# The source-row gathers of a graph attention kernel read their indices from the whole table instead of a per-chunk copy

## The reference, cut to what matters

```
src, dst = (edge_index[0], edge_index[1])
q = (x @ Wq + bq).reshape(n, H, D)
k = (x @ Wk + bk).reshape(n, H, D)
v = (x @ Wv + bv).reshape(n, H, D)
qi = q[dst]
kj = k[src]
vj = v[src]
alpha = jnp.sum(qi * kj, axis=-1) / jnp.sqrt(jnp.float32(D))
m = jax.ops.segment_max(alpha, dst, num_segments=n)
ex = jnp.exp(alpha - m[dst])
denom = jax.ops.segment_sum(ex, dst, num_segments=n)
a = ex / (denom[dst] + 1e-16)
out = jax.ops.segment_sum(a[..., None] * vj, dst, num_segments=n)
```

## Time and profile before

| | |
|---|---|
| median of 3 runs | 1489.38 us (1484.93 to 1494.15) |
| time of the profiled execution | 1499.95 us |
| its span, first to last instruction | 1498.1 us |
| mean granted TensorE clock | 0.932 of full speed |
| edge stage, first gather to the last tiles (71 to about 845 us) | about 774 us |
| all that follows | about 653 us |

### The profile page before, as it was taken

The page is one execution under the profiler, slowest core; times in us unless marked ns, Lnnn a source line. Parts: engine busy times, 40 slices in busy tenths (PEclk is TensorE's granted clock), DMA queues, the critical chain, the costliest instruction groups (busy, mean ns, idle before and its releaser), DMA issues. The chain is left out here.

```text
span 1498.1 us, 24128 instructions
## 1 busy us (share of the span) xinstructions
PE 1242.9 (83%) x6835; PEld 959.2 (64%) x6835; DVE 1068.4 (71%) x2557; ACT 807.4 (54%) x2534; POOL 927.2 (62%) x883
## 2 busy tenths in 40 slices
PE   7988776676776766667767889999999999999999
PEld 3444544444444444444445558889888998999998
DVE  7646877777778776768767888877766655656655
ACT  1365766666667666566655845556443244344443
POOL 3365666666666656666666546776676567667665
PEclk9998889999889898789887989999999999999999
DMA  7476766666666666666666030110100000000002
GB/s 225 164 229 203 224 201 171 194 196 191 186 184 203 185 187 178 182 183 181 185 178 179 8 105 29 29 50 12 30 22 15 8 22 15 8 22 15 1 12 76
DMA packets 74072, 175.40 MB, mean 117 GB/s; under 512 B 11500, under 2 KB 36651, under 8 KB 73945
## 3 DMA queue, kind: packets, MB, share of 16 engines
q0 software_dynamic: 37632, 124.28, 29.4%
q1 hardware_dynamic: 34641, 48.25, 10.0%
q10 hardware_dynamic: 1672, 1.33, 0.3%
HBM read 159.91 MB, written 13.91 MB: 116 GB/s over the span
## 5 line engine op out<-in xcount | busy, mean ns | idle before, releaser
L691 POOL DMA_INDIRECT ring<-kv_rows,idx x464 | 469.0, 1011 | 297.0 <-issue 116.6
L765 ACT ACTIVATE ring<-ring 128x64 f32<-128x64 f32 x1800 | 442.1, 336 | 15.0 <-issue 13.2
L1291 POOL TENSOR_TENSOR wm<-k_gf,wm 128x512 fp32r<-128x512 f32 (+2 forms) x224 | 258.9, 1159 | 144.1 <-DVE wm L1792 144.1
L1390 ACT ACTIVATE k_gf<-psF,k_scT 128x512 f32<-128x512 f32 (+2 forms) x224 | 162.1, 724 | 252.2 <-PE psF L1561 248.9
L811 PE MATMUL psA<-ring,oh 128*128 128x260 f32 x912 | 276.7, 432 | 7.1 <-DVE k_acc L1017 6.1
L785 PE MATMUL psQ<-k_q,ohT 128*128 x1392 | 228.6, 305 | 60.7 <-issue 56.0
L1792 DVE CAST wm<-k_gf 128x512 fp32r<-128x512 f32 (+2 forms) x224 | 159.5, 719 | 155.8 <-ACT k_gf L1390 155.8
L983 DVE TENSOR_TENSOR prod<-psQ,ring 128x512 f32<-128x512 f32 x232 | 157.6, 679 | 110.6 <-remote 68.5
L785 PEld LDWEIGHTS psQ<-k_q,ohT 128*128 128x128 bf16 x1392 | 131.8, 105 | 119.8 <-issue 88.7
L811 PEld LDWEIGHTS psA<-ring,oh 128*128 128x128 f32 x912 | 179.8, 219 | 35.8 <-ACT ring L765 6.5
L1023 DVE TENSOR_REDUCE alpha<-prod 128x8 f32<-128x512 f32 x232 | 155.8, 672 | 0.2
(11 more groups left out here) (284 smaller groups left out, 2607.3 us busy)
## 6 DMA issues: line engine op xcount, KB each, us to landing
ohT<-step_destinations SPq DMA_DIRECT2D x29, 512.0 KB
ring<-kv_rows,idx POOLq DMA_INDIRECT x464
kv_rows<-kvst SPq DMA_DIRECT2D x25, 260.0 KB, 2.6
we<-in_L_ffn_W SPq DMA_DIRECT2D x16, 256.0 KB, 2.7
residual<-qst SPq DMA_DIRECT2D x25, 128.0 KB
xs<-in_x SPq DMA_DIRECT2D x2, 1024.0 KB, 9.1
resin<-residual SPq DMA_DIRECT2D x4, 512.0 KB
we<-in_L_ffn_Wo SPq DMA_DIRECT2D x8, 256.0 KB, 2.8
```

Source lines behind the costliest of these rows:

```text
L691: nc.gpsimd.indirect_dma_start(out=ring[:, LT * (j % CP) + k, j // CP:j // CP + 2, :].rearrange("p t e -> p (t e)"), out_offset=None, in_= ...
L765: last = nc.scalar.activation(row[:, 0:D], row[:, 0:D], ACT.Copy, scale=row[:, D:HW_])
L1291: nc.gpsimd.tensor_tensor(low[:, i % 2, m, 0:w], gf[:, n % 4, 0:w], high[:, i % 2, m, 0:w], ALU.subtract).then_inc(s_gl, 1)
L1390: nc.scalar.activation(gf[:, n % 4, 0:cols(g)], ps, ACT.Relu, bias=bias, scale=scale).then_inc(s_ev, 1)
```

## The change

The gathers name their index column in the whole table `k_srcI`, column `LT * step + k`, instead of a column of the copy. The tile `idx`, the function `places`, its 29 activations, the semaphore `s_idx` and the two waits (POOL's for the copy, ACT's for the landed gathers) are gone. All else in the program is as it was; tiles allocated behind `idx` lie 128 bytes lower in each partition.

```
-        idx = sb("idx", [P, 2, W], I32)
...
-                cc, par = CR * i + j // CP, j // CP % 2
-                if j % CP == 0:
-                    pool.wait_ge(s_idx, cc + 1)
...
-                        in_offset=bass.IndirectOffsetOnAxis(ap=idx[:, par, LT * (j % CP) + k:LT * (j % CP) + k + 1], axis=0)
+                        in_offset=bass.IndirectOffsetOnAxis(ap=keep["srcI"][:, LT * step + k:LT * step + k + 1], axis=0)
...
-            def places(cc, par, fresh):
-
-                if not fresh:
-                    act.wait_ge(s_kv[CP - 1], 16 * LT * (cc - 1))
-                nc.scalar.activation(idx[:, par, :], keep["srcI"][:, bass.ds(W * cc, W)], ACT.Copy).then_inc(s_idx, 1)
...
-            places(0, 0, True)
...
-                if j % CP == 1 and live(i, j - 1, fresh, -CP):
-                    places(CR * i + j // CP + 1, (j // CP + 1) % 2, fresh and j < CP)
```

More of the change, by code:

```diff
@@ L592, in attend @@
         s_set = sem("s_set")
-        s_idx, s_stc = sem("s_idx"), sem("s_stc")
+        s_stc = sem("s_stc")
         s_kv = [sem(f"s_kv{k}") for k in range(CP)]
```

## The result

The changed kernel takes 1479.59 us (median of 8 runs, 1478.32 to 1481.59), the kernel before, beside it, 1491.72 us (8 runs, 1484.93 to 1495.19). The ratio is 0.9933, 95% interval 0.9910 to 0.9957: faster by 0.67%, where 1.23% was forecast. It is the 0.67% that this document has to explain: the two profiled executions differ by just what was forecast, 1498.1 us of span before and 1478.5 us after, 19.6 us less. The 1479.59 us lie at the upper edge of the forecast's own range, 1461 to 1480 us, and the gain falls where the prediction had put 0.44 (within 1%), not where it had put 0.46 (over 1%).

The account below looks back on a forecast made before the run. A ring of waits, paced by POOL's runs and pauses, was taken to bound the 774 us edge stage. Only DVE's 19 us counted: 1499.95 to 1481 us, ratio 0.9873, so 1471 us on the median; range 1461 to 1480 us.

Parts of the forecast that it names:

- POOL's pauses as the clock of the stage: Edge stage: POOL's runs of eight gathers (10.0 us) and a pause, four steps done, set the pace of the ring.
- The waits replaced by shorter ones: Chunk starts: without the index wait, a pause of 3.99 us becomes one like those of 1.94 to 2.37 us.
- The price by POOL: POOL's 17 index waits, 55.2 us: twelve long ones give 23.0 us, five others 4.3 us, sum 27 us.
- The sign that was to mean wrong: Profile after: runs of ten and more gathers with DVE chunks of over 28 us beside them would refute the prediction.
- The gather price: POOL's gathers from the 464-column table: still 0.946 us in the median, no gain or loss taken.
- the ACT copies: ACT's 29 index copies of 0.20 us go: 5.8 us, costed at nothing, worth 5.8 us at most.
- the data: DVE's wait before its product: gathered data isn't late, so an earlier gather gives DVE nothing directly.
- the 19 us: Edge stage by DVE's walk: all 28 chunks at 25.20 us in place of 25.89, 28 x 0.69 us shorter.
- Effect and cause the other way round: Rival: DVE, PE and ACT are slow for another reason, the index wait only shows it; 1483 to 1490 us, chance 0.29.
- The rule of the Trainium skill: Only the DVE/GpSimd port pair contends, so gathers can't hold PE or ACT; POOL's pauses would be effect, shorter ones give nothing.
- Longer runs, slower kernel: Rival: without index waits POOL's runs lengthen and others wait; 12 chunks paying 3.7 us give 1514 us, chance 0.10.
- The dearer table: Rival: the wide table costs 0.05 us more a gather, 23 us on POOL; 1493 us, chance 0.07.

Follow-up runs that it names:

- late copy: Kernel before, with ACT's index copy one place later, behind eight more activations, POOL's wait kept: 1546.10 us, ratio 1.0403, where the kernel before took 1487.36 us.
- table alone: Kernel before, gathers reading the whole table, copy and waits kept: ratios 1.0004, 1.0005, 0.9991 (before about 1350 us) and 0.9987 (1484.92 us, before 1485.18).

## Why the direction was right and the size was not

**POOL's pauses as the clock of the stage: borne out where a wait is made longer.** The doses of the wait are 0, 38.8, 55.2 and 127.2 us, and DVE's chunk goes 24.78 to 25.13, 25.36, 25.89 and 27.31 us with them; one profile each, and the steps below 127.2 us, 0.23 and 0.53 us, are of the size of the 0.35 us between profiles of the changed kernel. The late copy's chunk is made up of POOL's rows: 16 gathers of 0.986 us in the mean with 0.30 us between them are 20.6 us, and its pauses behind the first gather, 185.0 us, are 6.6 us a chunk, 27.2 us in all.

**The waits replaced by shorter ones: right.** The price by POOL took the sum to be there 1.9 us before a gather that waited for the copy; behind step 24, DVE's addition of that sum began 1.35 to 1.53 us ahead of all ten such gathers of over 1.2 us of wait, so it was there at least that much earlier. At the starts of the chunks after, the pauses are 2.4 us at most, but for 4.99 us at the start of chunk 1, which had been 4.66 us for the copy. Of the 55.2 us, (96.0 + 42.5 + 5.8) - (62.2 + 35.4 + 13.4) = 33.3 us came back in other waits (35.4 and 13.4 us are PE's and the remote ones of before), under the 35 us of the forecast, and 6.0 us more as issue (122.6 against 116.6). The idle time fell by 16.5 us, not by the 20 us or more that was forecast; but of the pauses over 1.2 us, 148.7 - 127.5 = 21.2 us went, between DVE's 19 and POOL's 27. DVE's chunks were to be near 25.2 us from end to end, with no series of 27 us. The mean is right (25.13 us), and the series is gone, but the evenness isn't there: single chunks of 27.2 to 28.3 us remain, four of 28, where there were seven of 27.0 us or more. The sign that was to mean wrong, a run of ten with a chunk of over 28 us beside it, stands there once, at the second chunk.

**The gather price, the ACT copies, the data: right.** The median is 946 ns from either index tile (949 ns in the table alone), and the table alone measures 1.00 in both forms, in four sets.

**The step that failed is the 19 us, read from one execution and carried over as a ratio.** The prediction took 28 x 0.69 us from the profiled execution, made 1499.95 us into 1481, called it 0.9873, and applied that to the median of the runs, which gave 1471. As a statement on that execution it was right: 1480.36 / 1499.95 is 0.9869. But 1499.95 us wasn't a usual execution of the kernel before. It is 8.2 us over the median, and above all eight runs; the changed kernel's profiled execution, 1480.36 us, is 0.8 us over its own. Take the 8.2 us from 19.6, add the 0.8, and 12.2 us are left: the 12.1 us that was measured. That the long waits which made up the term were in part what made this execution a slow one fits this, but isn't shown: the kernel before was profiled only once in this form. The table alone, with all waits in place and a profiled time of 1483.19 us close to its median, shows what is more usual: waits of 3.7 us or more only five times, not twelve, and 28 x (25.36 - 25.12) = 7 us of chunk length over the change beside it. So in place of the 19 us the runs showed 12.1 us between the medians, beside 19.6 us between the two profiled executions. That the latter hit the forecast is in part luck: the other two profiles of the changed kernel (1480.1 and 1462.8 us) lie 18.0 and 35.3 us under the profile of before. It is luck too that the forecast's own absolute value, 1481 us for the changed kernel, is 0.1% off.

Even so there is no one true size. The same comparison gave 12.1, 18.1 and 3.2 us in three sets. The changed kernel itself took 1464.62 to 1472.97 us in one of them and 1478.32 to 1481.59 us in another, with no run in common. How often a chunk has a wait of 3.7 us or more differs too (twelve and five times in the two profiles with the wait in its old place), and that what the change can give differs with it is a guess.

**The rivals.** *Effect and cause the other way round* (1483 to 1490 us) falls by the late copy: an edit that adds no work and only puts the copy one place later costs 4%, where the rival expected 1.00. The rule of the Trainium skill behind it, page "SBUF — State Buffer", section "Who interferes with whom", isn't contradicted by that. What falls is what I drew from it. The runs show that POOL's pauses carry over to DVE through the waits between them; they don't show that a gather holds another engine. *Longer runs, slower kernel* (1514 us) falls: of the three profiles of the changed kernel the one with the most runs of ten or more, 20, is the fastest, with the smallest sum of pauses. The chunk that the rival was built on did stay slow, 28.3 us (29.63 before), with a run of ten gathers beside it; it is one chunk at the start. *The dearer table* (1493 us) falls by the 946 ns and by the ratios of the table alone.

**What stays open.** First, what makes the 1490 form, where POOL pauses about every eight gathers. The traces show one side of it. ACT's `nrow` waits for PE's second transpose (L818 before, L805 in the changed kernel). In the kernel before, the transpose that the `nrow` at 586.02 waited for was over at 582.52, and ACT was idle:

```profile
582.25 0.27 PE L818 MATMUL psM<-k_ident,stc 128*64 128x128 f32 x1
```

The same pair in the 1350 form (table alone):

```profile
400.80 0.27 PE L818 MATMUL psM<-k_ident,stc 128*64 128x128 f32 x1
```

```profile
401.10 0.27 ACT L750 ACTIVATE nrow<-psM 64x128 f32<-64x128 f32 x1 [2.38 <-PE psM L818]
```

3.50 us lie between end and start in the one, 0.03 us in the other. In the 1350 form all 29 `nrow` begin 0.03 to 0.04 us behind the transpose. In the kernel before, in the 1490 form, 13 of 29 come 1.0 to 5.1 us behind it, each with ACT idle, and each of these 13 begins in a pause of POOL or behind its last gather, 1.1 to 1.5 us after the gather before it had ended. In the changed kernel 14 of 29 come 1.5 to 4.6 us late, but six of these while POOL is still gathering. So PE's signals do arrive late in the 1490 form, often only in a pause of POOL; but a run of gathers is not enough to make them late, since in the 1350 form 416 gathers go one after the other and none is. (The ends of PE's instructions are modelled in the profile.) The cause isn't shown.

Second, whether in that form POOL's wait alone is what the change gains by. Set directly beside the table alone in their common set, the change is 3.0 us faster by the medians and 3.3 us by the means, with a standard error of 1.1 us: taking away copy and waits gains something there with the table already in place. ACT's own wait never held it, as said above, so of ACT's part only the 29 copies are left, 5.8 us of work; the gains of 12.1 and 18.1 us are more than that, the 3.2 us aren't. The late copy speaks for POOL's wait, but the runs that would part the two in the 1490 form all fell in the 1350 form. Nor was it tested there whether the tiles that lie 128 bytes lower in the changed kernel matter; in the 1350 form the change, with them, is at 0.9990. Nothing tried beats the changed kernel.

## What to carry to other kernels

A wait on a pacing queue for a copy of data that the engine could read where it lies can cost far more than the copy: here 0.20 us of work behind waits of up to 6 us, and 4% when the copy slipped by one place; and nothing measurable in the form in which the queue hardly waits. The size of such a gain is no property of the kernel alone: set the profiled execution beside the median before carrying a ratio over, and if it is the slowest of all, take the excess off the term first (here 19 - 8.2 = 10.8 us, for 12.1 us measured). Before a wait is put down to the engine that the profile names, look whether the very step that the wait needs had not ended long before. In a ring of waits, sum what is left of each pause and not what is removed: of 55 us taken away, 33 us came back in the waits for others.

## What the runs showed of the hardware

The same kernel takes 1350 or 1490 us. The tail is alike, 653 us at a granted clock of 0.98 (of 2.4 GHz) in both. The edge stage is 626 us at a clock of 0.98 in the profile of the table alone, and 754 to 774 us at 0.88 to 0.89 in those of the kernel before and after (739 us at 0.89 in the fastest profile of the changed kernel), with DMA moving 231 GB/s or 187 to 196 GB/s. Over the whole execution the mean clock of the kernel before is 0.98 to 0.99 in the one form, but for one run, and 0.92 to 0.95 in the other. The lower clock alone isn't the difference: PE's busy time in the stage is 497 us against 551 to 556 us, 54 to 59 us more, while the stage differs by 129 to 148 us, and POOL, which has 472 to 476 us of work in either, shows it as pauses. And the one run left out, in the last set, had a mean clock of 0.932 and took 1356.57 us, 5.5 us over the median of its set: as low a clock as in the 1490 form, in the 1350 form's time. What differs as plainly as the clock is how soon ACT follows PE: 0.03 to 0.04 us every time in the 1350 form, up to 5.1 us in the 1490 form.
